# The values of an attention quad formed in one piece of 48 products instead of three pieces of 16

## The reference

```python
Q, K, V = proj(query, W_q), proj(key, W_k), proj(value, W_v)
Q, K = _apply_rope(Q, emb_q), _apply_rope(K, emb_k)
scores = jnp.einsum('bhqd,bhkd->bhqk', Q, K) / jnp.sqrt(jnp.float32(D_K))
scores = jnp.where(mask == 0, jnp.float32(-jnp.inf), scores)
attn = jax.nn.softmax(scores, axis=-1)
ctx = jnp.einsum('bhqk,bhkd->bhqd', attn, V)
...
x = x + jnp.tanh(g_xattn[0]) * (ctx @ W_o.T)
x = x + jnp.tanh(g_ffn[0]) * experts(layernorm(x))   # 8 experts, each takes its top 56 rows of a batch
```

## Time and profile before

| what | value |
|---|---|
| three runs | 1839.09, 1839.38, 1833.33 us; median 1839.09 |
| the profiled execution | 1836.25 us |
| its span, first to last instruction | 1834.4 us |
| mean granted TensorE clock | 0.981 of full speed |
| TensorE busy, of the span | 95% |
| VectorE busy | 57% |
| ScalarE busy | 46% |
| the four periods of a batch read from 461.75 to 722.95 us | 65.28 to 65.32 us each |

### The profile page before, as it was taken

How to read it: one execution, slowest core, us unless ns; L and a number is a source line. 1 busy time by engine, 2 the same in 40 slices (tenths; PEclk the granted TensorE clock), 3 DMA queues, 4 the chain that set the end, 5 groups by cost and what they waited for, 6 DMA issues and landing times.

```text
span 1834.4 us, 28481 instructions
## 1 busy us (share of the span) xinstructions
PE 1740.8 (95%) x10502; PEld 1545.1 (84%) x10502; DVE 1038.9 (57%) x1786; ACT 839.2 (46%) x1482; POOL 235.4 (13%) x302
## 2 busy tenths in 40 slices
PE   7999999899999999983999999999999999999995
PEld 6898998677777877753999999999999999999995
DVE  6666667777887787754544535435445354453541
ACT  3223225777776877742433434424344243343430
POOL 0000002131231232122000102002020020010101
PEclk9999999999999999995999999999999999999998
DMA  6544547756755755523333535335343252353421
GB/s 242 224 173 186 189 156 220 182 126 153 178 147 135 183 150 134 141 87 96 115 104 103 150 109 143 103 103 151 106 121 127 106 149 104 101 150 109 124 92 20
DMA packets 76301, 251.90 MB, mean 137 GB/s; under 512 B 10784, under 2 KB 10784, under 8 KB 74928
## 3 DMA queue, kind: packets, MB, share of 16 engines
q1 hardware_dynamic: 64208, 216.55, 38.3%
q0 software_dynamic: 12000, 34.12, 7.9%
HBM read 188.01 MB, written 51.61 MB: 131 GB/s over the span
## 4 chain that ended last, share of the span: by engine, by line
PE 52%; POOL 1%; DVE 0%; issue 0%; DMA 0%; DVEq 0%; ACT 0%; POOLq 0%
PE gu_ps L1624 11%; PE gu_ps L1623 11%; PE gu_ps L1622 11%; PE y_ps L1641 6%; PE y_ps L1640 6%; PE y_ps L1639 6%; PE y_ps L1650 1%; PE gu_ps L1608 1%; POOL out L1482 0%; DMA xg<-xn_rows,gather_i 0%; POOL gather_i L1469 0%; POOL xg L1472 0%; DVE xs_lo L1557 0%; DVE y_cols L1584 0%; PE gu_ps L1668 0%
## 5 line engine op out<-in xcount | busy, mean ns | idle before, releaser
L1622 PE MATMUL gu_ps<-xs_hi,ws_hi 128*128 128x448 f32 x1024 | 370.3, 362 | 3.0 <-DVE xs_lo L1557 3.0
L1624 PE MATMUL gu_ps<-xs_hi,ws_lo 128*128 128x448 f32 x1024 | 371.9, 363 | 0.0
L1623 PE MATMUL gu_ps<-xs_lo,ws_hi 128*128 128x448 f32 x1024 | 371.8, 363 | 0.0
L1552 DVE TENSOR_TENSOR ws_lo<-w_raw,ws_hi 128x1024 fp32r<-128x1024 f32 x192 | 235.2, 1226 | 189.3 <-ACT ws_hi L1502 188.3
L1502 ACT ACTIVATE ws_hi<-w_raw 128x1024 fp32r<-128x1024 f32 x192 | 201.5, 1051 | 163.7 <-PE y_ps L1641 150.6
L1298 PEld LDWEIGHTS t_ps<-cst,sm 112*125 112x125 f32 x1536 | 205.0, 190 | 68.6 <-issue 29.3
L990 DVE CUSTOM_DVE_ANT_0 sm<-m_ps,mq 112x752 f32<-112x752 f32 x256 | 229.7, 935 | 34.2 <-PE m_ps L1282 33.8
L1298 PE MATMUL t_ps<-cst,sm 112*125 112x112 f32 x1536 | 233.3, 281 | 15.0 <-DVE e_t L998 11.3
L880 ACT ACTIVATE sm<-sm,least 112x752 f32<-112x752 f32 x256 | 234.7, 919 | 13.7 <-DVE least L990 12.7
L1622 PEld LDWEIGHTS gu_ps<-xs_hi,ws_hi 128*128 128x128 f32 x1024 | 192.0, 187 | 16.9 <-issue 3.3
L1623 PEld LDWEIGHTS gu_ps<-xs_lo,ws_hi 128*128 128x128 f32 x1024 | 192.7, 188 | 14.6
(11 more groups left out here) (153 smaller groups left out, 2438.6 us busy)
## 6 DMA issues: line engine op xcount, KB each, us to landing
w_raw<-wstream SPq DMA_DIRECT2D x192, 512.0 KB, 3.5
ks<-k_split SPq DMA_DIRECT2D x192, 188.0 KB, 5.4
k_split<-k_split SPq DMA_DIRECT2D x32, 752.0 KB, 3.4
v_rows<-v_out SPq DMA_DIRECT2D x16, 750.0 KB
vs<-v_rows SPq DMA_DIRECT2D x16, 750.0 KB
c_raw<-ctxT SPq DMA_DIRECT2D x7, 1500.0 KB, 13.0
qs<-q_hi POOLq DMA_DIRECT2D x64, 112.0 KB, 5.1
mq_raw<-maskq SPq DMA_DIRECT2D x7, 656.2 KB, 10.9
```

The costliest lines, as they stand in the source:

```text
L1552: nc.vector.tensor_tensor(w_lo[s][:], w_raw[s][:], w_hi[s][:], ALU.subtract).then_inc(wlo_done[s], 1)
L1622: nc.tensor.matmul(o, w_hi[s][:, w], xs_hi[:, c], start=(c == 0), stop=False)
L1623: nc.tensor.matmul(o, w_hi[s][:, w], xs_lo[:, c], start=False, stop=False)
L1624: mm = nc.tensor.matmul(o, w_lo[s][:, w], xs_hi[:, c], start=False, stop=(c == DC - 1))
```

## The change

TensorE now forms all three parts of a quad's values one after the other in slot 2 of the next quad, between T0 and T1, and nothing in slots 1 and 3. The products, their number and their order among themselves stay; so do the waits, which stand at the first part, and the signal, at the last. No other engine's program is changed.

```diff
                         def last_values():
-                            if t >= HG:
-                                values(b, t // HG - 1, t % HG - 1)
-                            elif not first:
-                                values(b - 1, NG - 1, t - 1)
+                            for part in range(HG - 1):
+                                if t >= HG:
+                                    values(b, t // HG - 1, part)
+                                elif not first:
+                                    values(b - 1, NG - 1, part)
...
                         turn_rows(b, t, 0)
-                        if t % HG:
+                        if t % HG == 2:
                             last_values()
                         turn_rows(b, t, 1)
```

## The result

The changed kernel takes 1849.36 us in the median of four runs (1848.98 to 1850.61), against 1839.24 before (1833.33 to 1839.63). The ratio is 1.0068, 95% interval 1.0051 to 1.0085: slower by 0.7%. The profiled execution took 1849.5 us, its span is 1847.7, against 1836.25 and 1834.4. Forecast were 1844.5 and a loss of 6.8 us in the spans; the loss is 13.3.

A forecast was written before the change was run, and what follows sets the result against it. TensorE was taken to lead, closely balanced with VectorE and ScalarE. Six periods (+5.1) plus batches 0 and 7 (+1.7) made +6.8: 1843.1 us profiled, 1845.9 from the median, 1844.5 taken between; range 1828 to 1859.

The forecast's parts named there:

- a loss of 2 to 14 us: The prediction's own case for the whole kernel, chance 0.53, a third of it put above 9.2 us.
- What bounds the kernel: In attend, TensorE leads with 62.7 of 65.3 us, but VectorE (52.1) and ScalarE (48.8) are closely balanced with it.
- The saving of TensorE: V of 48 costs 2.6 us against 3 x 1.1: 0.7 a quad, 22 us, plus 7.8 of waits, if nothing else is late.
- Quad 1: Slots 4 to 7: VectorE works gapless behind T2(6), 9.38 us, so slot 7 gains nothing; T2(6) and T2(8) each +0.65.
- Quad 2: Slots 8 to 11: slot 11's scores wait for masks behind VectorE's T2(10); T0(10) -0.1, T2(10) +1.35, T2(11) +1.3.
- the walk: One batch of attend followed with traced step times against batch 6: period 66.15 instead of 65.3 us, +0.85.
- Quad 3: Slots 12 to 15: T2(13) +0.6, T2(14) +2.1, slot 15 -1.2, T2(15) +0.9, T2 of the next slot 0 +0.85.
- Batches 0 and 7: First batch from slot 5 on and last batch: 0.85 us taken for each (from -1 to +3), +1.7.
- The signs: Trace after: V one row, T2(6) to T2(8) 9.4 us, slot 11 unchanged, e_t waits 40 us or more, period 66.15.
- The first: Rival: TensorE is the bound and all else keeps up, 1810 us, or half of it, 1825; chance 0.13 together.
- The second: Rival: VectorE and ScalarE idle while V of 48 runs, about 1.1 us on ScalarE; +23, 1860 us; chance 0.20.

The follow-up runs named there:

- after_tiles: Changed kernel with VectorE emptying tiles 0 and 1 of slot 6 (not 1 and 2) and tile 0 of slot 10 (not 2): 1839.14 us, 0.9991 to before.
- v48_end: Changed kernel with the V piece of 48 in slot 2 behind T2 instead of between T0 and T1: 1854.40 us, 1.0082 to before.
- after_tile10: Changed kernel with VectorE emptying tile 0 of slot 10 instead of tile 2: 1848.17 us, one execution.
- half_after_tiles: Changed kernel with ScalarE copying half of each of its tiles in slots 8 to 15, plus the tile exchange of after_tiles: 1830.62 us, one execution.
- v48_slot1: Changed kernel with the V piece of 48 between T0 and T1 of slot 1 instead of slot 2: 1852.27 us, 1.0069 to before.
- v24x2: Kernel before with V in two pieces of 24, in slots 2 and 3, each between T0 and T1: 1841.26 us, 1.0009 to before.
- v16_end: Kernel before with its three V pieces of 16 behind T2 instead of between T0 and T1: 1837.97 us, 0.9992 to before.

## Why the prediction was right, and where it was small

The side and the mechanism were as forecast; the size in the spans was half. The 0.53 for a loss of 2 to 14 us went to the right case, but most of that case was put below 9.2 us: 0.19 (a third of 0.53 is 0.18) was left for its upper part, where the result lies. Point by point, the delay against the kernel before in batch 6, from T2(0) (694.63 after, 685.52 before, so 9.11 is taken off):

| point | forecast | measured | from |
|---|---|---|---|
| T0(3) | +1.3 | +1.33 | 705.11 and 694.67 |
| T2(3) | +0.2 | +0.25 | 706.65 and 697.29 |
| T0(6) | -0.9 | -0.77 | 719.28 and 710.94 |
| T2(6) | +0.65 | +0.74 | 723.42 and 713.57 |
| T2(8) | +0.65 | +0.75 | 732.81 and 722.95 |
| T2(10) | +1.35 | +1.66 | 740.45 and 729.68 |
| T2(11) | +1.3 | +1.67 | 743.91 and 733.13 |
| T2(13) | +0.6 | +0.91 | 749.90 and 739.88 |
| T2(14) | +2.1 | +2.52 | 754.58 and 742.95 |
| T2(15) | +0.9 | +1.45 | 758.14 and 747.58 |
| T2(0) of the next | +0.85 | +1.45 | 761.38 and 750.82 |

**What bounds the kernel.** Right. TensorE's busy share led, and saving its time brought a loss, since ScalarE and VectorE were the ones kept waiting.

**The saving of TensorE.** V of 48 is 2.48 us as in the one row that showed it, and the waits for `c_r` are gone. The saving is there where nothing waits: from T0 to the scores it takes 3.39 us with V of 48 (699.00 to 702.39) and 1.88 with V of 16 (686.62 to 688.50), against 0.79 without, so 3 x 1.09 - 2.60 = 0.67 a quad, forecast 0.7. TensorE's busy time in a period falls by only 0.32 us and not by four times that, since the waits inside rows took its place. What decided the side was that the forecast did not take this saving for time gained.

**Quad 1.** Right in the chain: T2(6) to T2(8) takes 9.39 us, forecast 9.38. after_tiles shows the cause: the masks of slot 6 start 1.12 us sooner and the quad is 1.12 shorter. v48_end is a second way to the same 21.6 us.

**Quad 2.** The named cause, slot 11's scores behind the masks, is in the trace at 742.71 and 743.48, and after_tile10 shows that it is 0.40 of the 0.92. The share that the walk carried too low comes in at T0(10): 0.1 earlier was forecast, 736.24 is 0.1 to 0.2 later. It waits for ScalarE's E1(9), which started at 735.54, 0.70 before, where I had counted 0.59; and V starts 0.59 behind that tile, not 0.52. So ScalarE's part of the walk was undersized. half_after_tiles shows that with ScalarE's work cut and the masks earlier nothing of the loss is left.

**Quad 3.** It gives back 0.22 where I had 0.4: slot 15 gained 1.07 and not 1.2.

**Batches 0 and 7** were the term that was taken and not worked out. From the same first `turn_parts` (312.57 and 312.58) the kernel after is 2.65 late at slot 8 of batch 1, where the forecast's terms give 0.85 + 0.65 = 1.5; 7.2 more in five periods, against 4.25; and 3.2 more to the last `turn_parts` (809.72 and 822.77), against 1.05. In batch 7 quad 0, which has no projections, alone costs 1.30 us (12.26 before, 13.56 after). The sum is 13.05 against 6.8. Not all of the 2.65 can be laid to the change's waits: TensorE's granted clock was 0.50 from 327.7 to 337.5 in the kernel after, and in the kernel before only from 361.9 to 365.4, 5.1 and 1.7 us of full speed lost. Up to 3.4 us of the 13.05 may be this, by this one pair of traces; the 1.44 us a period are read at a clock of 1.00 and hold without it.

**The signs.** V as one row with nothing before it, T2(6) to T2(8) at 9.4 us, slot 11 as long as before (3.45 and 3.46 from T2(10) to T2(11)), waits for `least`, and a period between 65 and 67.2 all came. TensorE's waits for `e_t` rose from 15 to 28.5 us and not to 40; the rest stands inside rows.

**The rivals.** The first, everything gained, is out. The second, idle time of ScalarE behind V, named the missing part, but it was not the only bound, so the price of 23 us was too high. ScalarE waits 1.20 us there; the prediction says 1.1, though the terms it gives (0.62 and 1.35 of work, E1 at 3.65) make 1.7. It is less in the trace since ScalarE comes to E0(10) late, behind E2(9).

The Trainium skill, in Perfetto Trace Analysis, Matmuls, asks for groups that rotate so that one is emptied under the next; the trace agrees in its sign: tiles wait for ScalarE 14.1 us in all instead of 3.7, among them T0(10) and T1(13), ahead of which a V is gone. What the Trainium skill says in TensorEngine Tiling (Array Packing), Key Properties, of a drain at a change of tiling mode can't be told apart in the times here: the 0.67 us of a quad include it, and no run changes the number of switches alone.

## What to carry to other kernels

An engine at 95% busy is not a bound that can be lowered alone, when others at 75 to 80% run in step with it through two or three short buffers: look at what each of them holds to do while the long block runs, and at what is queued behind the work that this block delays. Filler work belongs where its engine would wait anyway, in a size that the others can cover, and that place differs from quad to quad: the same joined piece, put into slot 1 of a quad, gained 0.5 us in quad 0 and lost 1.1 in quad 2. A steady loop's marks, read quad by quad, tell apart what a run's time can't, and let forms be combined.

## What the runs showed besides

**The granted clock.** Near the start of the attention, up to 421 us, and in v48_slot1 in its last quads too, TensorE's granted clock fell to 0.50 for 3 to 14 us at a time, 1.2 instead of 2.4 GHz, at different moments in each kernel; from 425 to 700 us it was 1.00 in all of them. Rows of that time, of the kernel after, the kernel before and v48_slot1, where the same products take 1.02 to 1.29 us (x8) and 0.96 (x16) at full clock:

```profile
332.75 1.89 PE L1298 MATMUL t_ps<-cst,sm 112*125 112x112 f32 x8
```

```profile
363.11 1.72 PE L1322 MATMUL o_ps<-e_t,vs 125*32 125x224 f32 x16
```

```profile
754.82 2.00 PE L1298 MATMUL t_ps<-cst,sm 112*125 112x112 f32 x8
```

Shortly before, TensorE had stood idle in the first two: 1.03 us up to 327.31 in the kernel after, 1.60 us up to 360.45 in the kernel before. Ten us of it cost up to 5 us of full speed, half of what the change costs in the medians, which is one more reason to compare forms by their quad times.

**The loads of `ks`.** Up to 420 us, in batch 0 and the first slots of batch 1, TensorE's scores waited for them by very different amounts: 0.8 us after, 2.7 in v48_end, 4.5 in v24x2 and after_tiles, 5.7 in v16_end, as the waits of TensorE have it (here v16_end):

```profile
PE m_ps L1282 <- DMA ks<-k_split: 5.7, 2, 4.5
```

The kernel before has no wait of that name, but 1.6 us without a named releaser at the scores of slot 1 of batch 1 (360.45), which need loads of `ks` and of `qs`. The loads of `ks` stand on SP's queue behind the waits for the stores of the first stage. In v16_end's profiled execution, with these waits and a clock of 0.50 for some 10 us in all, it takes 68.55 us from the first `turn_parts` to that of slot 4 of batch 1, where the kernel before takes 62.14; that is more than all it gains later, 0.4 us a batch. Whether it is the queue or the stores was not tried.
